# A layer of state-space mixer, experts, linear attention and experts on one core: the state-space stage reordered into eight phases, with both parts of the values in one stationary operand

## The reference, cut to what matters

```
proj = x @ W_in.T                       # values 512, gate 512, B 32x128, C 32x128, dt 32
val  = silu(causal_conv4(val) + b)      # 512 channels
cum  = cumsum(-softplus(dt + bias) * exp(A_log))        # per batch and head
M[l, m] = (C[l] . B[m]) * exp(cum[l] - cum[m])  for m <= l     # 256 x 256 per batch and head
Y    = (M @ val + D * val) * silu(gate)
out  = Y @ W_out.T
```

## Time and profile before

| | |
|---|---|
| median of 3 runs | 1497.19 us (1496.82 to 1499.1) |
| the profiled execution's own time | 1496.01 us |
| its span from the first to the last instruction | 1494.2 us |
| mean granted TensorE clock | 0.989 of full speed |
| TensorE busy | 1437.9 us, 96% of the span, 8520 matmuls |
| VectorE, ScalarE, GpSimd busy | 897.2, 863.9 and 817.1 us |
| chain that ended last | 58% on TensorE, 5% issue, 5% ScalarE, 4% VectorE, 4% GpSimd |

### The profile page before, as it was taken

How to read it: one execution, slowest core, us unless ns; L and a number is a source line. 1 busy time by engine, 2 the same in 40 slices (tenths; PEclk the granted TensorE clock), 3 DMA queues, 4 the chain that set the end, 5 groups by cost and what they waited for, 6 DMA issues and landing times.

```text
span 1494.2 us, 24410 instructions
## 1 busy us (share of the span) xinstructions
PE 1437.9 (96%) x8520; PEld 1248.1 (84%) x8520; DVE 897.2 (60%) x1713; ACT 863.9 (58%) x1735; POOL 817.1 (55%) x685
## 2 busy tenths in 40 slices
PE   7799999999999999999999999999999999999998
PEld 5589898898976778887789999999999987778886
DVE  6776766767664443434766767677666754443434
ACT  5566666666655343333677777777777755343332
POOL 4744444444434555553576666766676634555553
PEclk9999999999999999999999999999999989999999
DMA  2133332332311111111232123212222011111111
GB/s 83 32 66 79 68 69 67 67 78 68 69 53 32 43 43 53 42 53 32 65 82 63 51 57 74 63 49 56 63 63 63 15 42 33 43 42 53 42 53 39
DMA packets 48603, 82.48 MB, mean 55 GB/s; under 512 B 4256, under 2 KB 29984, under 8 KB 48288
## 3 DMA queue, kind: packets, MB, share of 16 engines
q1 hardware_dynamic: 48544, 81.70, 21.1%
HBM read 80.38 MB, written 1.31 MB: 55 GB/s over the span
## 4 chain that ended last, share of the span: by engine, by line
PE 58%; issue 5%; ACT 5%; DVE 4%; POOL 4%; DMA 0%; DVEq 0%; POOLq 0%; ACTq 0%; SPq 0%
PE ps L243 19%; PE ps L245 18%; PE ps L244 18%; POOL planes_lo L393 1%; POOL ms_b_lo L393 1%; ACT q L1317 1%; POOL qk_lo L393 1%; PE ps L294 1%; PE ps L301 1%; DVE qsum L1455 1%; ACT planes_hi L1322 1%; DVE f_h L1081 0%; DMA fw_raw<-ffn_w 0%; ACT qk_hi L389 0%; ACT fh_hi L389 0%
## 5 line engine op out<-in xcount | busy, mean ns | idle before, releaser
L393 POOL TENSOR_TENSOR ms_a_lo<-m_a,ms_a_hi 128x384 fp32r<-128x384 f32 x128 | 129.9, 1015 | 200.2 <-ACT ms_a_hi L389 200.2
L1081 DVE TENSOR_TENSOR f_h<-f_sc,ps 128x512 f32<-128x512 f32 x112 | 76.4, 682 | 182.5 <-POOL f_sc L1013 182.5
L243 PE MATMUL ps<-xn_hi,fgu_hi 128*128 128x512 f32 x448 | 177.3, 396 | 5.2 <-DVE f_h L1081 5.2
L245 PE MATMUL ps<-xn_hi,fgu_lo 128*128 128x512 f32 x448 | 178.2, 398 | 0.0
L244 PE MATMUL ps<-xn_lo,fgu_hi 128*128 128x512 f32 x448 | 177.0, 395 | 0.0
L1083 DVE TENSOR_TENSOR fh_lo<-f_h,fh_hi 128x512 fp32r<-128x512 f32 x112 | 107.2, 957 | 98.3 <-ACT fh_hi L389 98.3
L962 ACT ACTIVATE f_s<-ps 128x512 f32<-128x512 f32 x112 | 66.7, 597 | 161.2 <-PE ps L245 161.0
L1013 POOL TENSOR_TENSOR f_sc<-f_s,coef_r 128x512 f32<-128x512 f32 x88 | 114.0, 1296 | 67.5 <-ACT f_s L962 67.5
L389 ACT CAST fh_hi<-f_h 128x512 fp32r<-128x512 f32 x112 | 69.1, 617 | 124.9 <-DVE f_h L1081 124.8
L393 POOL TENSOR_TENSOR fd_lo<-fw_raw,fd_hi 128x256 fp32r<-128x256 f32 x56 | 52.1, 930 | 125.7 <-ACT fd_hi L389 125.7
L243 PE MATMUL ps<-xn_hi,aw_hi 128*128 128x512 f32 x256 | 108.8, 425 | 7.4 <-DVE bmat_lo L696 7.4
(11 more groups left out here) (276 smaller groups left out, 4901.1 us busy)
## 6 DMA issues: line engine op xcount, KB each, us to landing
fw_raw<-ffn_w SPq DMA_DIRECT2D x56, 384.0 KB, 3.0
rows_a<-a_rows_d SPq DMA_DIRECT2D x64, 256.0 KB, 4.8
wconv_raw<-b_conv SPq DMA_DIRECT2D x16, 513.0 KB, 3.6
aw_raw<-a_heads SPq DMA_DIRECT2D x32, 256.0 KB, 5.2
wvo_raw<-b_vo SPq DMA_DIRECT2D x16, 512.0 KB, 3.6
rows_b<-b_rows_d SPq DMA_DIRECT2D x32, 256.0 KB, 4.8
wqk_raw<-b_qk SPq DMA_DIRECT2D x16, 256.0 KB, 4.8
x<-xT SPq DMA_DIRECT2D x2, 512.0 KB, 4.9
```

The costliest lines, as they stand in the source:

```text
L243: nc.tensor.matmul(o, w[0], v[0], start=first, stop=False, skip_group_check=True)
L245: return nc.tensor.matmul(o, w[1], v[0], start=False, stop=last, skip_group_check=True)
L393: return nc.gpsimd.tensor_tensor(dst[1], src, f32(dst[0]), ALU.subtract).then_inc(sem(done_sem), 1)
L1081: nc.vector.tensor_tensor(f_h[:, c], f_sc[:, c], ps[:, 2 + c, :], ALU.mult).then_inc(sem("f_h"), 1)
```

## The change

The stage is cut into 8 phases instead of 4 groups: a phase is 8 heads and two of the four batches, 16 units, and it has two halves of 4 heads (8 units).

- `valz` now holds, for the 4 heads of a half, the `hi` parts at their 64 columns and the `lo` parts in the other 64. A value product becomes 3 matmuls of 256 columns: this operand against `ms_hi` and `ms_lo` of the first blocks, and once against both parts of the last block side by side. The half's sum comes out on 64 partitions and its `lo` part on the other 64.
- So each half needs a new sum per batch (`a_sum_dve`: three VectorE instructions on 64 partitions) and a copy of the `lo` part to the right partitions (`a_lo_act`), in the units 1 and 2 of the next half. The gate follows once per phase in unit 2, `ys` in units 3 and 4, the output products in units 7 and 10 of the next phase. The products with a zero block are gone.
- A head's B and C are projected for two batches only, one projection per unit as before, three units ahead of the score (`LEAD`); all 8 heads' weights stay in SBUF for the second phase of a group. Four heads' weights are split before the stage, not two.
- Exponents and decays are made one unit ahead.
- The values are transposed straight from `valT` in unit 4 of the phase before, copied to SBUF (`val_tok`), and split in units 2 and 11 by ScalarE and GpSimd; the copy `stage` is gone.
- The convolution of the fourth tile moves from GpSimd to VectorE.

The core of the diff:

```
+A_HALF = A_GROUP // 2
+STEPS = A_HEADS * CHUNKS
+ALL_UNITS = 2 * STEPS
+PHASES = A_TILES * CHUNKS
+PHASE_UNITS = ALL_UNITS // PHASES
+HALF_UNITS = PHASE_UNITS // 2
...
+SUM_UNITS, YS_UNIT, OUT_UNITS = (1, 2), 3, (7, 10)
+VALZ_UNITS, T_UNIT, AWO_UNIT = (2, 11), 4, 13
...
+        LEAD = 3
...
-        def a_value_pe(pe, g, u):
-            j, b = u // BATCH, u % BATCH
-            pe.wait_ge(sem("a_m_split"), UNITS * g + u + 1)
-            if u == 0:
-                pe.wait_ge(sem("valz_split"), 2 * g + 2)
-            o, l0, t = ps[:, 6 + b // 2, :], (b % 2) * SEQ, 2 * b
-            ms = at(ms_a, slice(None), u % 3)
-            mm3(half_view(o[:, l0:l0 + SEQ]), at(valz, slice(None), j, t), tuple(first_m(v) for v in ms),
-                j == 0 and b % 2 == 0, False)
-            mm3(o[:, l0 + P:l0 + SEQ], at(valz, slice(None), j, t + 1), at(ms, slice(None), slice(P, 2 * P)),
...
+        def of_step(k):
+            return k // (2 * A_GROUP), k // A_GROUP % 2, k % A_GROUP
...
+        def a_project_pe(pe, q):
+            k, s = q // 2, q % 2
+            g, c, j = of_step(k)
+            if s == 0:
+                pe.wait_ge(sem("aw_split"), head_of(k) + 1)
+            if q >= 2:
+                pe.wait_ge(sem("bc_split"), q - 1)
+            for kt in range(KT):
+                ins = mm3(ps[:, s, :], at(aw, slice(None), j, kt, s), at(xn, slice(None), kt, cols(c)), kt == 0, kt == KT - 1)
             ins.then_inc(sem("a_p_done"), 1)
...
+        def a_state_pe(pe, u):
+            k, b = u // 2, u % 2
+            p, l0 = k % 2, b * SEQ
             if u >= 2:
+                pe.wait_ge(sem("a_m_done"), u - 1)
+            if b == 0:
+                pe.wait_ge(sem("bc_split"), 2 * k + 2)
+            s = ps[:, 4 + b, :]
             mm3(first_m(s), at(bmat[p], slice(None), slice(l0, l0 + P)), halves(at(cmat[p], slice(None), slice(l0, l0 + SEQ))), True, False)
             mm3(s[:, P:2 * P], at(bmat[p], slice(None), slice(l0 + P, l0 + SEQ)),
                 at(cmat[p], slice(None), slice(l0 + P, l0 + SEQ)), False).then_inc(sem("a_s_done"), 1)
...
+        def a_value_pe(pe, u):
+            n, j, b = u // HALF_UNITS, u // 2 % A_HALF, u % 2
+            pe.wait_ge(sem("a_m_split"), u + 1)
+            if u % HALF_UNITS == 0:
+                pe.wait_ge(sem("valz_split"), n + 1)
+            if j == 0 and n > 0:
+                pe.wait_ge(sem("y_read"), 2 * (n - 1) + b + 1)
+                pe.wait_ge(sem("lo_read"), 2 * (n - 1) + b + 1)
+            o, ms = ps[:, 6 + b, :], at(ms_a, slice(None), u % 3)
+            for i, m in enumerate(ms):
+                nc.tensor.matmul(half_view(o[:, 0:SEQ]), valz[:, n % 2, j, 2 * b], first_m(m), start=j == 0 and i == 0,
+                                 stop=False, skip_group_check=True)
+            nc.tensor.matmul(half_view(o[:, P:TRI]), valz[:, n % 2, j, 2 * b + 1], ms_a[2][:, :, u % 3, P:2 * P], start=False,
+                             stop=j == A_HALF - 1, skip_group_check=True).then_inc(sem("a_y_done"), 1)
...
+        def a_phase_pe(pe, p):
+            for n in range(PHASE_UNITS):
+                u = PHASE_UNITS * p + n
                 if u > 0:
+                    a_state_pe(pe, u)
+                if u + LEAD < ALL_UNITS:
+                    a_project_pe(pe, u + LEAD)
+                if n == T_UNIT and p + 1 < PHASES:
+                    a_transpose_pe(pe, p + 1)
+                if n in OUT_UNITS and p > 0:
+                    a_out_pe(pe, p - 1, OUT_UNITS.index(n), 3)
                 if u >= 2:
+                    a_value_pe(pe, u - 2)
...
         def a_prepare_rest_act(act):
+            for h in range(FILLED):
+                a_fill_act(act, h)
...
+        def a_fill_act(act, h):
+            act.wait_ge(sem(f"aw_loaded{h % 2}"), 16 * (h // 2 + 1))
+            split_hi(at(aw, slice(None), h % A_GROUP), aw_raw[:, h % 2], "aw_hi")
...
+        def a_project_act(act, q):
+            k, s = q // 2, q % 2
+            act.wait_ge(sem("a_p_done"), q + 1)
+            nc.scalar.copy((bmat, cmat)[s][k % 2][0][:], ps[:, s, :]).then_inc(sem("bc_hi"), 1)
...
+        def a_lo_act(act, n, b):
+            act.wait_ge(sem("a_y_done"), HALF_UNITS * (n + 1) - 2 + b + 1)
+            if n >= 2:
+                act.wait_ge(sem("lo_added"), 2 * (n - 2) + b + 1)
+            nc.scalar.copy(y_lo[half_rows(n % 2), b * SEQ:(b + 1) * SEQ],
+                           ps[half_rows(1 - n % 2), 6 + b, 0:SEQ]).then_inc(sem("lo_read"), 1)
...
+        def a_phase_act(act, p):
+            for n in range(PHASE_UNITS):
+                u = PHASE_UNITS * p + n
+                k, b = u // 2, u % 2
+                if u + 1 < ALL_UNITS:
+                    a_decays_act(act, u + 1)
+                if u + LEAD < ALL_UNITS:
+                    a_project_act(act, u + LEAD)
+                act.wait_ge(sem("a_m_done"), u + 1)
+                split_hi(at(ms_a, slice(None), u % 3), m_a[:, b, :], "a_m_hi")
+                if p > 0 and n in SUM_UNITS:
+                    a_lo_act(act, 2 * p - 1, SUM_UNITS.index(n))
+                if n - HALF_UNITS in SUM_UNITS:
+                    a_lo_act(act, 2 * p, SUM_UNITS.index(n - HALF_UNITS))
+                if n == VALZ_UNITS[0]:
+                    a_valz_act(act, 2 * p + 1)
+                if n == YS_UNIT and p > 0:
+                    a_y_act(act, p - 1)
+                if n == T_UNIT + 1 and p + 1 < PHASES:
+                    a_tokens_act(act, p + 1)
+                if n == VALZ_UNITS[1] and p + 1 < PHASES:
+                    a_valz_act(act, 2 * p + 2)
+                if b == 1 and fill_of(k) is not None:
+                    a_fill_act(act, fill_of(k))
+                if n == AWO_UNIT and p % 2 == 0:
+                    act.wait_ge(sem("awo_loaded"), 16 * (p // 2) + 16)
                     split_hi(at(awo, slice(None)), awo_raw[:], "awo_hi")
...
+        def a_sum_dve(dve, step, n, b):
+            rows, t, c = half_rows(n % 2), n // 4, n // 2 % 2
+            l0 = c * CHUNK + b * SEQ
+            y, o = yT[rows, b * SEQ:(b + 1) * SEQ], ps[rows, 6 + b, :]
+            dve.wait_ge(sem("a_y_done"), HALF_UNITS * (n + 1) - 2 + b + 1)
+            step(nc.vector.scalar_tensor_tensor(y, valT[rows, t, l0:l0 + SEQ], a_d[rows, t:t + 1], o[:, 0:SEQ], ALU.mult, ALU.add))
+            nc.vector.tensor_tensor(y[:, P:SEQ], y[:, P:SEQ], o[:, SEQ:TRI], ALU.add).then_inc(sem("y_read"), 1)
+            dve.wait_ge(sem("y_read"), 2 * n + b + 1)
+            dve.wait_ge(sem("lo_read"), 2 * n + b + 1)
+            nc.vector.tensor_tensor(y, y, y_lo[rows, b * SEQ:(b + 1) * SEQ], ALU.add).then_inc(sem("lo_added"), 1)
...
+        def a_gate_dve(dve, p):
+            dve.wait_ge(sem("lo_added"), 4 * p + 4)
+            nc.vector.tensor_tensor(yT[:], yT[:], gateT[:, p // 2, cols(p % 2)], ALU.mult).then_inc(sem("y_gated"), 1)
...
+        def a_exponents_dve(dve, u):
+            k, b = u // 2, u % 2
+            dve.wait_ge(sem(f"a_rows_loaded{k % 3}"), 16 * (k // 3 + 1))
+            if u >= 2:
+                dve.wait_ge(sem("a_m_done"), u - 1)
+            exponents_dve(e_a[:, b], rows_a[:, k % 3, b, :], ncum_a, 2 * of_step(k)[1] + b, head_of(k)).then_inc(sem("a_bounded"), 1)
...
+        def a_phase_dve(dve, step, p):
+            for n in range(PHASE_UNITS):
+                u = PHASE_UNITS * p + n
+                k, b = u // 2, u % 2
+                if u + 1 < ALL_UNITS:
+                    a_exponents_dve(dve, u + 1)
+                if u > 0 and u - 1 + LEAD < ALL_UNITS:
+                    a_project_dve(dve, u - 1 + LEAD)
+                dve.wait_ge(sem("a_s_done"), u + 1)
+                dve.wait_ge(sem("a_e_done"), u + 1)
                 if u >= 2:
+                    dve.wait_ge(sem("a_m_split"), u - 1)
+                nc.vector.tensor_tensor(m_a[:, b, :], ps[:, 4 + b, 0:TRI], e_a[:, b, :], ALU.mult).then_inc(sem("a_m_done"), 1)
+                if p > 0 and n in SUM_UNITS:
+                    a_sum_dve(dve, step, 2 * p - 1, SUM_UNITS.index(n))
+                if n - HALF_UNITS in SUM_UNITS:
+                    a_sum_dve(dve, step, 2 * p, SUM_UNITS.index(n - HALF_UNITS))
+                if p > 0 and n == SUM_UNITS[1]:
+                    a_gate_dve(dve, p - 1)
+                if p > 0 and n == YS_UNIT + 1:
+                    a_y_dve(dve, p - 1)
+                if p > 0 and n in OUT_UNITS:
+                    a_out_dve(dve, p - 1, OUT_UNITS.index(n), 3)
...
+        def a_fill_pool(pool, h):
+            split_lo(pool, at(aw, slice(None), h % A_GROUP), aw_raw[:, h % 2], "aw_hi", h + 1, "aw_split")
...
+        def a_valz_pool(pool, n):
+            pool.wait_ge(sem("valz_hi"), n + 1)
+            nc.gpsimd.tensor_tensor(valz_diagonal(n % 2, 1), val_of(n % 2), f32(valz_diagonal(n % 2, 0)),
+                                    ALU.subtract).then_inc(sem("valz_split"), 1)
...
+        def a_phase_pool(pool, p):
+            for n in range(PHASE_UNITS):
+                u = PHASE_UNITS * p + n
```

(51 more changed lines are left out.)

410 lines of the change are left out of this document (142 added, 268 removed).

## The result

The changed kernel takes 1520.6 us (median of 4 runs, 1520.1 to 1522.1) against 1497.0 (1496.0 to 1499.1) for the kernel before: a ratio of 1.016, 95% interval 1.0148 to 1.0172. It is slower, as forecast, but by 23.6 us and not by 8, and outside the range of 1474 to 1515. The profiled execution took 1520.1 us with a span of 1518.3.

The account below looks back on a forecast made before the run. TensorE's matmul stream was taken to bound the stage. From 1496.0 us, -40.4 of savings gave 1455.6; waits of +38.3 and slow clock of +9.8 made 1503.7, 1505 as the median, range 1474 to 1515.

Parts of the forecast that it names:

- Value products, outputs, transposes, start and tail: TensorE's stage and both its ends: -34.2, -1.4, +0.4, -3.7, and -1.5 for low-part waits gone; -40.4 us, giving 1455.6.
- The tail: Stage end, last score with a projection ahead to last value product: 6.0 us instead of 10.5, so -4.5.
- The start: Before the stage: first value product 2 us earlier, bounded by -4 and +2, with one more whole unit (2.5) bounded.
- The waits: Unit 4's score in each half waits for VectorE's sums and gate: 7 x 3.35 + 8 x 1.85 = +38.3 us.
- The clock: TensorE at half clock behind about 8 in 10 of the seven long first-half waits, none behind shorter ones: +9.8 us.
- The sum: Whole kernel: 1455.6 + 38.3 + 9.8 = 1503.7, with 1.2 more for the median of the runs: 1505 us.
- The shorter waits bring the clock down too: Rival: half clock also behind the second halves' waits, 8 x 0.8 x 1.75 more, 1516 us; chance 0.10.
- The clock stays up: Rival: TensorE's waits come as computed but no half clock follows, about as before, 1495 us; chance 0.17.
- no collision: Rival: VectorE's additions don't collide with GpSimd, waits of 1.55 and 0.85 too short for the clock, 1475 us; chance 0.22.
- The signs asked for in the profile: Stage: value products 0.36, units 2.50, waits each half 3.2 and 1.7, additions about 0.9 us, PEclk 0.85 to 0.95.

Follow-up runs that it names:

- The kernel without the low sums: Changed kernel with the copy and addition of each sum's low part left out, so the output lacks them: 1455.7 us, ratio 0.9721.
- early copy and late gate: Changed kernel with ScalarE's copy of the sum's low part right behind the decays and the gate one unit later: 1453.0 us, ratio 0.9703.
- the kernel with PSUM: Changed kernel with the sum's low part copied to a free PSUM bank instead of SBUF, so the addition reads one SBUF operand: 1480.3 us, ratio 0.9884.
- the kernel kept busy: Changed kernel with 10 matmuls of zeros ahead of each of the 15 late scores, so TensorE works while it waits: 1495.9 us, ratio 0.9992.

## Why the prediction was right in sign and wrong in size

- **Value products, outputs, transposes, start and tail** (-40.4, so 1455.6): held as a sum. The kernel without the low sums measured -42.2, and the one with early copy and late gate, which does the whole work and has no late score, -44.1. The sum held in part by luck. Over the stage the median spacing of the scores went from 2.77 to 2.44 us, so the units alone are worth 122 x 0.33 = -40.3 where -34.2 stood, and the rest -2 to -4 where -6.2 stood. The tail came as forecast: from the last score with a projection in front of it, at 452.51, to the end of the last value product at 458.54 it takes 6.0 us. The start did not: the first value product came at 71.71 in the profiled execution, 1.3 us earlier than before and not 2, and at 73.12 in that of the kernel with PSUM, so this term is nothing that the runs bear out. No term named that TensorE would wait 4.06 us for `cmat_lo` until 67.74, ahead of the stage, and run at half clock until 73.69.
- **The waits** (+38.3): right to a tenth. The idle time recorded is 37.6; by the spacing of the scores, which is what the walk forecast, a first half's score is 3.51 us late (walked: 3.35), a second half's 4.59 - 2.44 = 2.15 (1.85) and the very first 2.25: 7 x 3.51 + 7 x 2.15 + 2.25 = 41.9. Their mechanism was right too: additions at 0.88 (walked: 0.93), held by GpSimd until 0.28 us before their end, with the gate at 1.10 behind GpSimd's split of 0.92.
- **The clock** (+9.8): this is the step that failed, "I expect the fall after about 8 in 10", 3.5 us each, and "For the shorter waits of 1.85 in the second halves I count none." Measured about 25 (the kernel kept busy) to at most 28 us (the windows). The first halves fell 7 times in 7, and in 5 of these the clock stayed down for 6.8 us, since a second 3.4 followed the first: 41 us at half clock, up to 20 lost, where 9.8 stood. The second halves fell 5 times in 7: 17 us at half clock, up to 8.5 lost, some of it past 450, where 0 stood. A piece of 3.4 us lost at most the 1.7 that was forecast; there were 17 pieces instead of 5.6.
- **The sum** with measured terms. From the first value product to the last score the changed kernel takes 383.0 us and the one with early copy and late gate 315.5. Of the 67.5 between them 41.9 are the late scores, which leaves 25.6 for the clock, and 1497.0 - 44.1 + 41.9 + 25.6 = 1520.4, for 1520.6. Against the forecast the base is 4 us lower, the waits are 4 higher, and the clock is 16 higher: the clock is the miss.
- **The rivals.** "The shorter waits bring the clock down too", 1516 at a chance of 0.10, named what happened; even so it left out that a fall can last twice as long. "The clock stays up", 1495, is what the kept-busy kernel measures (1495.9), and "no collision", 1475, is near what the one with PSUM does (1480.3). In the earlier trace rows stood three idle stretches of 1.86 to 1.95 us, of which two had a fall behind them. I used them as if they had said that a wait of 1.9 us is safe, though they said 2 in 3. They were not all either: the trace of the kernel before has seven between 1.8 and 2.4 us, with half clock behind three (ends at 717.77, 754.36 and 1212.26) and not behind four (456.59, 497.69, 1240.79, 1282.36; two of these are 2.31 us long). At 3 in 7 the second halves would have brought 8 x 0.43 x 1.75 = 6 us.
- The signs asked for in the profile were all there: 0.35 and near 2.50 us, one wait per half, additions of 0.9 behind a GpSimd start, and a granted clock of 0.93, inside 0.85 to 0.95. The last did not fit my own sum: a clock of 0.95 over the 373 us of the stage is already 0.05 x 373 = 19 us, where I had 9.8. Put side by side, the two would have shown that one of them was wrong.

## What to carry to other kernels

Where TensorE is the bound, a recurring wait of about 2 us costs its length once and up to the same again in clock (here 42 and 25 us): price it with the falls that the trace already shows for stretches of that length, all of them and the short ones too, and make the range from none to all of them. A VectorE instruction with two SBUF operands is placed ahead of the GpSimd instruction that it would meet, or gets one operand from PSUM; moving a 0.4-us copy by half a unit was worth 55 us here, and the gate's move by one unit 12 more. Work that hangs on a group's end is spread over units so that no unit's queue on VectorE exceeds what the bounding engine leaves.
